# Half of each layer normalisation moved from the vector engine to the scalar engine, in a two-layer transformer tower

## The reference

```python
def _layernorm(x, axis=-1, eps=1e-05):
    m = jnp.mean(x, axis=axis, keepdims=True)
    v = jnp.var(x, axis=axis, keepdims=True)
    return (x - m) / jnp.sqrt(v + eps)
...
h = _layernorm(h + _L0_attn_ref(h, ...))   # causal attention, 8 heads of 32, with a rank-one bias
h = _layernorm(h + _L0_ffn_ref(h, ...))    # inner layer norm, attention with 32 heads of 8, experts by position, Gelu
h = _layernorm(h + _L1_attn_ref(h, ...))   # gated linear attention, 4 heads
h = _layernorm(h + _L1_ffn_ref(h, ...))    # 8 experts, top 2 by a learned gate
```

## Time and profile before

| | us |
|---|---|
| median of 3 runs | 1624.34 |
| lowest, highest | 1619.41, 1625.54 |
| profiled execution, its time | 1620.52 |
| its span | 1618.6 |
| PE busy | 1162.4 |
| DVE busy | 744.5 |
| ACT busy | 486.2 |
| mean granted clock of TensorE | 0.837 of full |

### The profile page before, as it was taken

One profiled execution on the slowest core, in us unless ns is written; L12 is line 12 of the kernel. 1 busy time (PEld: TensorE's weight loads), 2 busy tenths in 40 slices (PEclk: granted clock), 3 DMA queues, 4 the chain that ended last, 5 costly groups with the idle time before them and its releaser, 6 DMA issues. The chain is left out here.

```text
span 1618.6 us, 22238 instructions
## 1 busy us (share of the span) xinstructions
PE 1162.4 (72%) x7926; PEld 786.0 (49%) x7926; DVE 744.5 (46%) x1836; ACT 486.2 (30%) x1123; POOL 163.8 (10%) x219
## 2 busy tenths in 40 slices
PE   1111888778898868888777989777514999999930
PEld 0001465444665445664544655554412666666620
DVE  7995334575534674335575555424230222222236
ACT  1000133244454423254224554232000333333310
POOL 3681000000000000000000000000043000000033
PEclk8555899799999998599787999786556999999975
DMA  7011002100012000011000020000691111111023
GB/s 239 5 22 48 26 2 68 37 14 1 1 53 72 1 27 1 1 57 55 1 14 1 27 85 1 13 27 0 216 343 65 33 36 35 36 33 33 30 59 107
DMA packets 65482, 78.01 MB, mean 48 GB/s; under 512 B 14960, under 2 KB 57600, under 8 KB 65248
## 3 DMA queue, kind: packets, MB, share of 16 engines
q1 hardware_dynamic: 61040, 63.08, 12.1%
q0 software_dynamic: 4336, 13.50, 2.5%
HBM read 55.86 MB, written 20.71 MB: 47 GB/s over the span
## 5 line engine op out<-in xcount | busy, mean ns | idle before, releaser
L1254 DVE TENSOR_REDUCE mx<-ps 128x2 f32<-128x512 f32 (+1 forms) x320 | 197.5, 660 | 151.3 <-PE ps L765 111.1
L1076 ACT ACTIVATE pt<-ps 128x512 f32<-128x512 f32 (+1 forms) x320 | 167.4, 573 | 279.2 <-PE ps L787 201.6
L1687 PE MATMUL x_ps<-x_w,x_xtT 128*128 x312 | 143.4, 603 | 0.8 <-ACT x_xtT L1727 0.5
L1698 PE MATMUL x_ps<-x_w,x_hT 128*128 x624 | 141.2, 379 | 2.1 <-ACT x_hT L1742 2.1
L1833 DVE COPY x_raw<-x_ps 128x512 f32<-128x512 f32 x78 | 54.0, 692 | 168.2 <-PE x_ps L1687 168.2
L1742 ACT ACTIVATE x_hT<-x_ps,x_b1c 128x128 f32<-128x128 f32 x312 | 84.9, 383 | 142.2 <-PE x_ps L1705 142.2
L1698 PEld LDWEIGHTS x_ps<-x_w,x_hT 128*128 128x128 f32 x624 | 115.6, 190 | 16.8 <-issue 2.7
L777 PE MATMUL ps<-q,k 32*128 32x256 f32 x512 | 70.8, 349 | 49.9 <-DVE mx L1254 39.8
L787 PE MATMUL ps<-mrow,pick 128*128 128x512 f32 x256 | 101.1, 479 | 0.0
L713 POOL COPY vpad<-v 128x64 f32<-128x64 f32 x64 | 13.6, 243 | 815.8 <-PE ps L826 662.0
L777 PEld LDWEIGHTS ps<-q,k 32*128 32x128 f32 x512 | 43.7, 200 | 100.6 <-DVE mx L1254 60.1
(11 more groups left out here) (340 smaller groups left out, 2103.8 us busy)
## 6 DMA issues: line engine op xcount, KB each, us to landing
wexp<-in_L_ffn_w SPq DMA_DIRECT2D x16, 1024.0 KB, 5.4
x_w<-in_L_ffn_W SPq DMA_DIRECT2D x16, 1024.0 KB
x_slots<-s_zero POOLq DMA_DIRECT2D x1, 4992.0 KB, 20.1
x_xt<-x_slots SPq DMA_DIRECT2D x39, 128.0 KB, 2.2
y_slots<-x_y SPq DMA_DIRECT2D x39, 128.0 KB, 1.7
ha<-h SPq DMA_DIRECT2D x16, 256.0 KB, 3.0
h<-s_out SPq DMA_DIRECT2D x32, 64.0 KB, 1.8
x<-hb SPq DMA_DIRECT2D x8, 256.0 KB, 2.5
```

What stands on the lines that cost most here:

```text
L1076: sc.activation(pt[v.index % PT_RING][:, 0:wide], ps[2 + v.index % 2][:, 0:wide], ACT.Exp)\
L1254: v.tensor_reduce(mx[:, u.group % 2, 0:blocks, u.n], bank[:, 0:blocks * (P if u.causal else T)].rearrange("p (b k) -> p b k", b=blocks), A ...
L1687: last = mm(ps[h][:, :], xtT[:, i % 2, c, :], w1[:, bass.ds(expert, 1), c, h * HALF:(h + 1) * HALF], start=c == 0, stop=c == DC - 1)
L1698: last = mm(ps[4 + (i - 1) % 2][:, 0:D], hT[:, (i - 1) % 2, f, :], w2[:, bass.ds(last_expert, 1), f, :], start=f == 0, stop=f == FT - 1)
```

## The change

DVE normalises blocks 0 and 1 of each tile, ACT blocks 2 and 3, at all 16 places. ACT computes Identity(scale * x + bias) with two operands per partition: scale is the root, bias is -mean * root. DVE works out this bias for both blocks in one instruction of 128x2 (`shifts`; in Y2 two of them, for `xn` and h1) and signals it. ACT waits for that signal once in each Y2 and twice in each Y1b, so 12 times. Whoever reads a normalised tile now waits for both halves: PE before its transposes, SP before the store, and DVE itself where it later writes or reads the tiles again (`normed_by_act`): for h1 and h3 right behind its own half, for h2 a few steps later.

```diff
@@ main_loop
+    shift = sb("shift", [P, 2, 2])
+
+    NORMS = [use for s, p in plan.stages for use in {"Y2": [("xn", p), ("h1", p)], "Y1b": [("h2", p), ("h3", p)]}.get(s, [])]
+
+    def normed(name, p):
+        return NORMS.index((name, p)) + 1
@@ sync, before the store of h3
                 sp.wait_ge(sg("h3"), p + 1)
+                sp.wait_ge(sg("normed"), 2 * normed("h3", p))
@@ tensor, y2 (and the same with "h2" in y1b)
             pe.wait_ge(sg("xn"), p + 1)
+            pe.wait_ge(sg("normed"), 2 * normed("xn", p))
             transposes(ob, "xn_t", p)
@@ scalar
+        asked = [0]
+
+        def normalised(src, dst, i, root):
+            if i == 0:
+                asked[0] += 1
+                act.wait_ge(sg("shifts"), asked[0])
+            for tb in range(2):
+                sc.activation(dst[:, 2 + tb, :], src[:, 2 + tb, :], ACT.Identity, bias=shift[:, i, tb:tb + 1],
+                              scale=root[:, 2 + tb:3 + tb]).then_inc(sg("normed"), 1)
+
@@ scalar, y2
             turned("p0", p)
-            yield from pause(7)
+            yield from pause(5)
+            normalised(yb, ob, 0, rs[0][:, 8:12])
+            yield
+            if p >= 2:
+                act.wait_ge(sg("x3_out"), 32 * (p - 1))
+            normalised(yb, hb[p % 2], 1, rs[1])
+            yield
@@ scalar, y1b, first steps
-            yield from pause(3)
+            yield
+            normalised(yb, hb[p % 2], 0, rs[1])
+            yield from pause(2)
             turned("h2", p)
@@ scalar, y1b, last steps
             turned("p2", p)
-            yield from pause(5)
+            yield from pause(4)
+            normalised(yb, hb[p % 2], 0, rs[1])
+            yield
@@ vector
         def normalised(src, dst, root):
-            for tb in range(NTB):
+            for tb in range(2):
                 s.mark(v.tensor_scalar(dst[:, tb, :], src[:, tb, :], mv[:, tb, 0:1], root[:, tb:tb + 1],
                                        ALU.subtract, ALU.mult))
             s.sync()
+
+        def shifts(i, root):
+            s.mark(v.scalar_tensor_tensor(shift[:, i, :], mv[:, 2:4, 0], -1.0, root[:, 2:4], ALU.mult, ALU.mult))
+
+        def normed_by_act(name, p):
+            dve.wait_ge(sg("normed"), 2 * normed(name, p))
@@ vector, y2
             s.step(v.tensor_tensor(r12, r1, r2, ALU.mult))
+            shifts(0, r12)
+            shifts(1, r1)
+            signal("shifts")
             yield
             normalised(yb, ob, r12)
             signal("xn")
@@
             normalised(yb, hb[p % 2], rs[1])
+            normed_by_act("h1", p)
             yield
@@ vector, y1b, first step (and the same before h3)
             moments(rs)
+            shifts(0, rs[1])
+            signal("shifts")
             yield
             normalised(yb, h, rs[1])
             signal("h2")
@@ vector, y1b, gate
             s.mark(v.tensor_scalar(gm, gz, 0.0, None, ALU.min))
+            normed_by_act("h2", p)
@@ vector, y1b, last step
             normalised(yb, h, rs[1])
             signal("h3")
+            normed_by_act("h3", p)
             yield
```

More of the change, by code:

```diff
@@ L988, in y1b @@
             pe.wait_ge(sg("h2"), p + 1)
+            pe.wait_ge(sg("normed"), 2 * normed("h2", p))
             transposes(hb[p % 2], "h2_t", p)
```

## The result

Over 20 runs each, the changed kernel takes 1627.18 us in the median (1623.29 to 1638.14) and the kernel before 1620.80 (1611.20 to 1627.12). The ratio is 1.0061, with a 95% interval from 1.0042 to 1.0080: **slower by 0.6%**, about 10 us. (The medians differ by 6.4 us, the ratio makes 9.9.) The median lies 1.2 us above the forecast of 1626 and within its range, but the case "slower by over 0.5%", given 0.13, is the one that the ratio speaks for. The profiled execution took 1623.29 us, its span 1621.6: it is the shortest of the 20.

A forecast was written before the change was run, and what follows sets the result against it. It took PE's waits for DVE and ACT between 165 and 1146 us as the only place to act. Terms 1.9 + 0.4 + 0.6 + 0.4 - 1.2 = +2.1 us on the 1624.34 median gave 1626 us, range 1618 to 1636.

The forecast's parts named there:

- ACT's pair: At each normalisation, ACT's two 128x256 ACTIVATEs take 1.1 us, bounds 0.84 and 1.2; one alone 0.6 us.
- The shift: DVE's added 128x2 bias instructions, ahead of ACT's half: 0.28 us in Y2 (two), 0.20 us at h2 and h3.
- xn, pair 0: ACT's exponentials and `acc` wait behind shifts and ACT's half, so PE's transposes come later: +1.9 us, bounds 0 and 2.5.
- xn, pair 1: DVE waits for ACT's half of h1 ahead of the next `mx`, delaying PE: +0.4 us.
- h2 and h3, pair 0, and h2, pair 2: The DVE `mx` or copy behind the shorter normalisation starts earlier: -0.4 us each.
- xn, pairs 2 and 3: Two shifts stand ahead of the `mx` PE waits for, the saving behind it: +0.3 us each.
- h3, pairs 1 and 2: One shift stands ahead of the `mx` PE waits for, the saving behind it: +0.2 us each.
- h2, pairs 1 and 3: PE waits for the tile itself; ACT's half ends about when the whole did: 0 us.
- The clock: TensorE's clock in the woven part: no sign expected; a mean 0.005 higher or lower gives 4.3 us either way.
- DVE's relief: Rival: DVE's 7.5 us saving comes through everywhere, giving 1617 us, or 1613 with clock; chance 0.11.
- ScalarE's half becomes the bound: Rival: ACT's half delays work behind it at eleven more calls, 9 us more, 1635 us; chance 0.17.
- The clock alone: Rival: with the steps as listed, TensorE's clock moves time 5 to 10 us either way, 1617 or 1636; chance 0.10.

The follow-up runs named there:

- again: The changed kernel, unaltered, timed once more beside the kernel before: median 1627.66 us, ratio 1.0050 to the kernel before.
- late: Changed kernel, with ACT's halves of xn and h2 placed one step later; h1 and h3 stay: 1628.14 us, ratio 1.0050 to the kernel before.
- not_p0: Changed kernel with all normalisations split except xn and h1 of pair 0: ratio 1.0008 to the kernel before.
- after: The profiled execution of the changed kernel, nothing further altered: 1623.29 us, span 1621.6.
- y2_only: Changed kernel with only xn and h1 of the four pairs split, h2 and h3 on DVE: 1627.03 us, ratio 1.0047 to the kernel before.
- only_p0: Changed kernel with only xn and h1 of pair 0 split, all others on DVE: ratio 1.0031 to the kernel before.
- wait_only_p0: Kernel before plus pair 0's shifts of Y2 and ACT's wait for them; DVE still normalises all blocks: ratio 1.0002 to the kernel before.
- xn_p0: Changed kernel with only xn of pair 0 split, all others on DVE: ratio 1.0021 to the kernel before.
- dose_p0: Only xn and h1 of pair 0 split, and ACT repeats its pair at xn four more times into scratch: ratio 1.0054 to the kernel before.
- before: The profiled execution of the kernel before, without the change: 1620.5 us, span 1618.6.
- same_as_before: The kernel before, unchanged, timed against itself: ratio 0.9992.
- y1b_only: Changed kernel with only h2 and h3 split, xn and h1 on DVE: 1623.30 us, ratio 0.9999 to the kernel before.
- y2_p1_to_p3: Changed kernel with only xn and h1 of pairs 1 to 3 split: ratio 1.0011 to the kernel before.
- double_not_p0: All split except xn and h1 of pair 0, and ACT computes each of its 14 pairs once more into scratch: ratio 1.0036 to the kernel before.

## Why the prediction was right in its steps and short in its size

- **The number.** 1626 hit 1627.18 in part by luck. The forecast of the rise was +2.1 us, and the medians rose by 6.4. It was set on a median of three runs, 1624.34, which over 20 runs is 1620.80. The two misses, 4.3 and 3.5 us, nearly cancel.
- **Its own sign of being wrong**, a change of more than 8 us from 165 to 1146 us: the last normalisation of the loop is aggregated at 1141.40 before and 1143.30 in the profile after, so +1.9, but at 1152.21 in `again`, +10.8. One trace passes and one fails.
- **ACT's pair**, forecast 1.1 us: 1.09 to 1.12 in the profile after, one alone 0.598. The upper bound from rows (0.63) and the value taken (0.6) hold. The Trainium skill, "ScalarE: Activation LUTs", section "What ACT_TABLE_LOAD costs", gave 585 ns and 1.08 us a pair: the trace agrees within 13 ns and 0.04 us.
- **DVE's two** in 0.73: as forecast. Busy time moved by 8.7 us (forecast some 10) and 15.9 (18 or 19), as overlaps are counted once. **The shift** was too cheap in the forecast: 0.20 and 0.28 us were taken, and where a `mx` stands behind it the places show +0.30 for one (h3 of pairs 1 and 2) and +0.37 for two (xn of pairs 2 and 3). The instructions are short (0.16 and 0.23 us), but what follows on DVE starts 0.32 to 0.38 us after the shift does. The signal took 0.09 us to reach ACT (253.89 to 253.98), where 0.05 was taken.
- **xn, pair 0**, forecast +1.9: +2.04 at the transposes of ob. In detail the step was wrong about which wait grows. It read PE's wait of 0.92 us as one for the `acc` that would move by 1.9 us, and put the transposes of `acc` 1.9 us later. They come 0.39 us later, 6.75 us behind the aggregation instead of 6.36: they start 0.10 us after DVE's division before and after, and it is the division that stands behind the shifts. `late`, where this is the only change ahead of them, shows the same 0.38. Then the values wait another 1.09 us for the next `acc`, which the forecast moved but didn't name as the limit.
- **xn, pair 1**, forecast +0.4, with a DVE wait for ACT ahead of the `mx`. The wait is there; in `not_p0`, where pair 0 does not disturb the clock ahead of it, DVE shows it as:

```profile
358.86 0.73 DVE L1347 TENSOR_SCALAR hb<-yb,mv,rs 128x256 f32<-128x256 f32 x2
360.78 1.29 DVE L1292 TENSOR_REDUCE mx<-ps 128x2 f32<-128x512 f32 x2 [1.19 <-ACT hb L1128]
```

  The `mx` starts 18.85 us behind the aggregation instead of 18.53; PE's transposes of ob stand at 21.20 instead of 21.06. So +0.15. In the profile after they stand at 22.25, but 0.96 of these 1.19 us were there already at PE's scores shortly before (18.69 instead of 17.73), where `not_p0`, with the same split, stands at 17.65; the account leaves them out.
- **h2 and h3, pair 0, and h2, pair 2**, forecast -0.4 each: 5.70 to 5.34, 6.72 to 6.45, 7.70 to 7.37, so -0.36, -0.27 and -0.33.
- **xn, pairs 2 and 3**, forecast +0.3 each: 6.83 to 7.20 and 7.11 to 7.47. **h3, pairs 1 and 2**, +0.2 each: 4.14 to 4.44 and 3.32 to 3.62. **h2, pairs 1 and 3**, 0: 4.31 to 4.23 and 4.32 to 4.33. For h3 of pair 3 there is no row: PE's next wait there is ended by a DMA. The places in this item and the one before are as forecast within 0.15 us.
- **The sum**: 2.04 + 0.15 - 0.96 + 0.73 + 0.60 - 0.07 = +2.5, forecast +2.1. The span of the profiled execution grew by 3.0.
- **The clock** is where the reasoning failed. The forecast said that the stalls ahead of slow stretches change by 0.2 to 0.4 us of 2 to 5, "so I expect no sign". It looked at stretches that were slow already, and not at the place that it had itself called dear, where PE had its full clock and would now stand for 1.31 and 1.09 us in a row instead of 0.92. There a half-rate stretch begins that the kernel before does not have: in all eight traces in which xn of pair 0 is touched (`after`, `again`, `y2_only`, `late`, `only_p0`, `wait_only_p0`, `xn_p0`, `dose_p0` at 1.91 to 1.97 us for the eight transposes) and in none where it isn't (`before`, `same_as_before`, `y1b_only`, `not_p0`, `y2_p1_to_p3`, `double_not_p0` at 1.09). At once it costs 0.8 us (2.85 less 2.04), in the trace of `again` 5 us more. What it costs over all runs is not shown. The steps leave 4 to 7 us, for which the clock is the candidate that is left, but `wait_only_p0` has the stretch and loses nothing that can be measured, and the profile after has the same mean clock up to pair 1 as the kernel before. The forecast allowed 4.3 us of clock with either sign.
- **The rivals.** DVE's relief does not come through: of 8.7 us of DVE time three places give back 0.96. "ScalarE's half becomes the bound" is answered by `double_not_p0` for the single pair of the change: its mechanism stands at xn of pair 0, as listed, and with a doubled pair at xn of pair 1 too. The Trainium skill, same page, "Rules for kernel authors", says to use VectorE and not ScalarE for multiplications and additions. The sign here agrees, and so do the two instructions (598 against 407 ns), but the loss at xn of pair 0 is made by the place of the wait and of the pair in ACT's queue (0.87 and 0.73 us). "The clock alone" is the rival nearest to what was left over, and it is not excluded.

What stays open: the 4 to 7 us beyond the steps; why `y2_only` (+7.6 us, with steps of 2.7) costs as much as it does, and `late` (+8.1 us, with steps of 2.5 - 1.5 + 2.26 = 3.3); and whether `wait_only_p0` got off by its smaller delay or within its interval of 0.2%.

## What to carry to other kernels

Before work is given to an engine that is idle two thirds of the time, look at what stands behind the new instruction in that engine's queue, and at what it waits for: here a wait for DVE's chain was put in front of exponentials that had been ready, and one place out of sixteen made 2.0 of the 2.5 us that the traces account for, while fourteen others together cost nothing that could be measured (at most 1.0031 by their interval). Splitting a tile between engines gains for the reader of the tile only if the slower half plus its hand-over (here 0.3 us of shift and 1.1 us) is shorter than the whole was (1.37 us). And look apart at a new stall where TensorE had its full clock: here a half-rate stretch began behind it each time, whose price in time these runs leave open. Last, a forecast of 2 us set on three runs that lie 6 us apart can hit its number by luck; judge it by its steps.

## What was not expected of the hardware

- Counted from the start of its own chain, a place mostly repeats between executions and kernels within 0.02 us (h2 of pair 0: 5.68 to 5.70 in eight traces where it isn't split, 5.34 to 5.36 in five where it is). It does not where the clock differs: PE's scores behind h3 of pair 0 stand at 4.14 in `before` and 5.03 in `same_as_before`. And the interval between two such places differs by up to 7 us between two traces of the same program (h3 of pair 0 behind h2: 68.09 and 75.12 in `before` and `same_as_before`), with different stretches of half clock between. Effects of tenths can be read from one trace where the clock is the same, effects of the clock only from many runs.
- How TensorE's clock stood in the first 165 us, in which PE is busy for 20 us, goes with 9 us of time in the changed kernel (the executions with the higher mean clock are the longer ones, in two batches of 20 and 12), and with none in the kernel before. Why is open.
- Where PE stood 0.4 us longer ahead of the transposes of `acc`, the full clock was gone at the transposes of ob: these eight took 1.97 us behind a wait of 1.30 us in `wait_only_p0`, and 1.09 us behind 0.92 in the kernel before.
